# Shift of a folded batch normalisation: added by VectorE in PSUM in place of a product of ones

## What is computed

```
h = relu(bn1(conv1(x1)))          # conv1: 256x256, one tap; bn1: h * scale + shift, per feature
h = bn2(conv2(h))                 # 17 taps along the nodes, 256x256 each
x_conv = relu(h + x1)
```

## Time and profile before

| | us |
|---|---|
| median of 3 runs | 1957.12 |
| lowest, highest | 1956.53, 1961.15 |
| the profiled execution: time, span of the core | 1959.8, 1958.0 |

### The profile page before, as it was taken

How to read it: one execution, slowest core, us unless ns; L and a number is a source line. 1 busy time by engine, 2 the same in 40 slices (tenths; PEclk the granted TensorE clock), 3 DMA queues, 4 the chain that set the end, 5 groups by cost and what they waited for, 6 DMA issues and landing times.

```text
span 1958.0 us, 35045 instructions
## 1 busy us (share of the span) xinstructions
PE 1883.0 (96%) x11046; PEld 1655.8 (85%) x11046; DVE 1430.3 (73%) x2972; ACT 1115.5 (57%) x2063; POOL 423.3 (22%) x378
## 2 busy tenths in 40 slices
PE   7999999996999899949999999999999999999997
PEld 6988999996999799948888888888888888888886
DVE  5888888885666788856777777777777777777774
ACT  6888888884666677734444444444444444444442
POOL 4766766764454100000000000000000000000000
PEclk9999999997999899969999999999999999999998
DMA  6778888875334688852121211212121212121200
GB/s 220 269 270 287 292 293 293 304 249 193 96 102 145 204 287 275 260 171 91 51 93 59 86 65 68 83 51 99 50 100 50 100 50 93 58 87 64 79 33 22
DMA packets 184169, 281.13 MB, mean 144 GB/s; under 512 B 14286, under 2 KB 126644, under 8 KB 179860
## 3 DMA queue, kind: packets, MB, share of 16 engines
q1 hardware_dynamic: 184084, 280.10, 42.3%
HBM read 178.60 MB, written 101.45 MB: 143 GB/s over the span
## 4 chain that ended last, share of the span: by engine, by line
PE 54%; issue 1%; DVE 1%; ACT 0%; DMA 0%; POOL 0%; POOLq 0%; ACTq 0%; SPq 0%; DVEq 0%
PE c_ps_g L1573 40%; PE c_ps_m L1551 5%; PE c_ps_m L1582 2%; PE c_ps_y L1606 1%; PE c_ps_m L1584 1%; PE c_ps_y L1666 1%; PE c_ps_m L1666 1%; PE c_ps_m L1583 1%; PE c_ps_s L1651 0%; PE c_ps_y L1667 0%; PE c_ps_m L1667 0%; DMA c_x<-x_t 0%; PE c_ps_s L1620 0%; PE c_ps_g L1623 0%; DVE c_wi_l L1517 0%
## 5 line engine op out<-in xcount | busy, mean ns | idle before, releaser
L1333 POOL TENSOR_TENSOR c_rstd<-c_var_eps,c_neg_half 128x4 f32<-128x4 f32 x32 | 32.2, 1007 | 1059.5 <-DVE c_var_eps L1473 1059.5
L1251 ACT ACTIVATE c_yo<-c_ps_y,c_shift,c_rstd 128x256 f32<-128x256 f32 x128 | 61.8, 563 | 169.4 <-DVE c_shift L1481 169.4
L1573 PE MATMUL c_ps_g<-c_ch,c_wi_l 128*128 128x512 f32 x384 | 154.5, 402 | 0.0
L1573 PE MATMUL c_ps_g<-c_nh,c_wi_l 128*128 128x512 f32 x384 | 153.3, 399 | 0.0
L1573 PE MATMUL c_ps_g<-c_xh,c_wh_l 128*128 128x512 f32 x384 | 152.3, 397 | 0.0
L1573 PE MATMUL c_ps_g<-c_xl,c_wh_h 128*128 128x512 f32 x384 | 152.1, 396 | 0.0
L1573 PE MATMUL c_ps_g<-c_xh,c_wh_h 128*128 128x512 f32 x384 | 151.7, 395 | 0.0
L1573 PE MATMUL c_ps_g<-c_ch,c_wi_h 128*128 128x512 f32 x384 | 151.7, 395 | 0.0
L1573 PE MATMUL c_ps_g<-c_cl,c_wi_h 128*128 128x512 f32 x384 | 151.6, 395 | 0.0
L1573 PE MATMUL c_ps_g<-c_nl,c_wi_h 128*128 128x512 f32 x384 | 151.2, 394 | 0.0
L1573 PE MATMUL c_ps_g<-c_nh,c_wi_h 128*128 128x512 f32 x384 | 150.9, 393 | 0.0
(11 more groups left out here) (219 smaller groups left out, 6143.1 us busy)
## 6 DMA issues: line engine op xcount, KB each, us to landing
w_spec<-a_spec SPq DMA_DIRECT2D x32, 1088.0 KB, 8.0
m_w<-w_spec SPq DMA_DIRECT2D x34, 1024.0 KB, 8.1
a_xt<-in_x_t SPq DMA_DIRECT2D x64, 256.0 KB, 3.4
a_xn<-in_x_n SPq DMA_DIRECT2D x64, 256.0 KB, 5.1
x_t<-a_x1t SPq DMA_DIRECT2D x64, 256.0 KB, 4.8
s_x<-x_t SPq DMA_DIRECT2D x64, 256.0 KB, 2.9
y_spec<-x_spec SPq DMA_DIRECT2D x64, 256.0 KB, 5.5
c_x<-x_t SPq DMA_DIRECT2D x32, 512.0 KB, 3.9
```

The lines of the kernel that those rows point to most:

```text
L1251: nc.scalar.activation(yo[:, b], ps_y[:, b], ACT.Identity, bias=shift[:, b:b + 1], scale=rstd[:, b:b + 1]).then_inc(s_yo, 1)
L1573: last = nc.tensor.matmul(out, stationary, moving, start=(count == 0), stop=(count == total - 1))
```

## The change

The product of ones is taken out. The first of conv1's twelve products now opens the bank (`start=True`), the others add to it. When conv1 of a unit is done, VectorE adds the shift, kept in float32 on all partitions in a tile of its own and broadcast over the two graphs, to the unit's bank in PSUM, in place, and signals a new semaphore `s_sh`; ScalarE's relu waits for that instead of for conv1. The addition is the first thing in VectorE's step, for unit i-2, ahead of the sums of unit i-4 and of `hl` of unit i-2. The preparation of the rows in `phase_a` falls away; the copy that made the rounded part now makes the kept tile.

```diff
@@ def kept(keep)
-    shift_rows = keep[:, 2 * half:3 * half].rearrange("p (b d) -> p b d", b=2).bitcast(F32R)
-    f = keep[:, 3 * half:3 * half + 2 * L].rearrange("p (s l) -> p s l", s=2).bitcast(F32R)
-    ones = keep[:, 3 * half + 2 * L:3 * half + 2 * L + P].bitcast(F32R)
-    return w_h, w_l, shift_rows, f, ones
+    f = keep[:, 2 * half:2 * half + 2 * L].rearrange("p (s l) -> p s l", s=2).bitcast(F32R)
+    return w_h, w_l, f
@@ phase_a, tiles (shift_h, shift_l, shift_m go)
@@ phase_a, scalar
                 if i == 18:
                     act.wait_ge(s_ch, 1)
-                    nc.scalar.activation(shift_h[:, :], rows[:, 1], ACT.Copy).then_inc(s_ch, 1)
+                    nc.scalar.activation(shift_kept[:, :], rows[:, 1], ACT.Copy).then_inc(s_ch, 1)
...
                 if i == 22:
                     nc.scalar.activation(f[:, 0], f_raw[:, :], ACT.Copy).then_inc(s_ch, 1)
-                    nc.scalar.activation(ones_kept, ones0[:, :], ACT.Copy)
@@ phase_a, vector
-                if i == 20:
-                    dve.wait_ge(s_ch, 2)
-                    nc.vector.tensor_tensor(shift_l[:, :], rows[:, 1], shift_h[:, :].bitcast(F32), ALU.subtract).then_inc(s_cn, 1)
...
-                if i == 24:
-                    nc.vector.tensor_scalar(shift_m[:, :], shift_h[:, :].bitcast(F32), mk[:, 0:1], None, ALU.mult).then_inc(s_cn, 1)
-                if i == 25:
-                    dve.wait_ge(s_cn, 10)
-                    for b in range(2):
-                        nc.vector.scalar_tensor_tensor(shift_rows[:, b], shift_l[:, :], mk[:, 1:2], shift_m[:, :], ALU.mult, ALU.add).then_inc(s_cl, 1)
@@ phase_spectrum
-        w_h, w_l, shift_rows, f, ones = kept(keep)
+        w_h, w_l, f = kept(keep)
...
+        s_sh = sem("shift_added")
@@ phase_spectrum, scalar
                 if live(2):
                     p, r = i - 2, (u - 2) % RING
-                    reached(act, s_c1, p + 1)
+                    reached(act, s_sh, p + 1)
                     reached(act, s_f, B * (p - 1))
                     nc.scalar.activation(hh[:, u % 2], ps_c[:, r], ACT.Relu).then_inc(s_hh, 1)
@@ phase_spectrum, vector
             def step(i, u, k, live):
+                if live(2):
+                    p, r = i - 2, (u - 2) % RING
+                    reached(dve, s_c1, p + 1)
+                    nc.vector.tensor_tensor(ps_c[:, r], ps_c[:, r], shift.rearrange("p (o d) -> p o d", o=1).to_broadcast([P, B, D]),
+                                            ALU.add).then_inc(s_sh, 1)
                 if live(4):
                     p = i - 4
@@ phase_spectrum, tensor
                     reached(pe, s_xl, p + 1)
                     reached(pe, s_hl, p - RING + 1)
-                    nc.tensor.matmul(ps_c[:, r].rearrange("p b d -> p (b d)"), ones,
-                                     shift_rows.rearrange("p b d -> p (b d)"), start=True, stop=False)
...
-                            last = nc.tensor.matmul(ps_c[:, r, b], xx[:, v, c, nodes], ww[:, c], start=False,
+                            last = nc.tensor.matmul(ps_c[:, r, b], xx[:, v, c, nodes], ww[:, c], start=(b == 0 and t == 0),
                                                     stop=(b == B - 1 and t == len(passes) - 1))
@@ kernel
         keep = ctx.enter_context(nc.sbuf_tensor("keep", [P, 8 * D], F32))
+
+        shift = ctx.enter_context(nc.sbuf_tensor("s_shift", [P, D], F32))
```

More of the change, by code:

```diff
@@ L63, in kept, with phase_a @@
     w_l = keep[:, half:2 * half].rearrange("p (c o) -> p c o", c=KD).bitcast(F32R)
-    shift_rows = keep[:, 2 * half:3 * half].rearrange("p (b d) -> p b d", b=2).bitcast(F32R)
-    f = keep[:, 3 * half:3 * half + 2 * L].rearrange("p (s l) -> p s l", s=2).bitcast(F32R)
-    ones = keep[:, 3 * half + 2 * L:3 * half + 2 * L + P].bitcast(F32R)
-    return w_h, w_l, shift_rows, f, ones
-def phase_a(nc, G, x_n, x_t, adj_t, w0, b_t, masks, x1_t, taps, taps_s, dft_w, w_spec, w_c1, bn1, dft_f, keep, s_spec, s_out, first_x, s_x):
+    f = keep[:, 2 * half:2 * half + 2 * L].rearrange("p (s l) -> p s l", s=2).bitcast(F32R)
+    return w_h, w_l, f
+def phase_a(nc, G, x_n, x_t, adj_t, w0, b_t, masks, x1_t, taps, taps_s, dft_w, w_spec, w_c1, bn1, dft_f, keep, shift_kept, s_spec, s_out, first_x, s_x):
     pairs = G // 2
@@ L118, in phase_a @@
         diag = sb("diag", [P, 2, KD, P])
-        shift_h = sb("shift_h", [P, D], F32R)
-        shift_l = sb("shift_l", [P, D])
-        shift_m = sb("shift_m", [P, D])
         f_raw = sb("f_raw", [P, L])
-        c_h, c_l, shift_rows, f, ones_kept = kept(keep)
+        c_h, c_l, f = kept(keep)
         rows = diag.rearrange("p s c n -> p s (c n)")
@@ L664, in load_filters, with phase_spectrum @@
                  ).then_inc(s_w[buffer], 16)
-def phase_spectrum(nc, G, x1_t, keep, x_spec, s_spec, s_out, x, s_x, w, w_spec, s_w):
+def phase_spectrum(nc, G, x1_t, keep, shift, x_spec, s_spec, s_out, x, s_x, w, w_spec, s_w):
     B = 2
@@ L1792 @@
         phase_a(nc, G, d["x_n"], d["x_t"], d["adj_t"], d["w0"], d["b_t"], d["masks"], x1_t, d["taps"], taps_s, d["dft_w"], w_spec,
-                d["w_c1"], d["bn1"], d["dft_f"], keep, s_spec, s_out, x, s_x)
+                d["w_c1"], d["bn1"], d["dft_f"], keep, shift, s_spec, s_out, x, s_x)
         x_spec = ctx.enter_context(nc.sbuf_tensor("x_spec", [P, KD, SLOTS, 2, G], F32))
         w = ctx.enter_context(nc.sbuf_tensor("m_w", [P, PAIRS, KD, CHUNKS, 2, 2, CW], F32))
-        phase_spectrum(nc, G, x1_t, keep, x_spec, s_spec, s_out, x, s_x, w, w_spec, s_w)
+        phase_spectrum(nc, G, x1_t, keep, shift, x_spec, s_spec, s_out, x, s_x, w, w_spec, s_w)
         phase_product(nc, G, x_spec, w, w_spec, y_spec, y_rest, keep, x, s_w)
```

## The result

The changed kernel takes 2040.89 us (median of 4, 2040.22 to 2041.82) against 1958.18 before (median of 4, one execution more than in the table of the kernel before): a ratio of 1.0422, 95% interval 1.0406 to 1.0439. It is slower by 82.7 us, and lies inside the predicted range. The profiled execution took 2041.13 us.

The account below looks back on a forecast made before the run. PE was taken to bound the kernel. 62 units x 1.48 us = 91.8, less 0.6 for the other two, gave +91 us: 1959.8 + 91 = 2051 profiled, median 2048, range some 2024 to 2063, top carried to 2078.

Parts of the forecast that it names:

- PE sets the pace, the others have room: Spectrum stage: PE is busy in all 40.00 us of each window, DVE and ACT in some 26.5, POOL in 19.5.
- The added wait: PE stands still from conv1's end to the b=0 sum's end, behind DVE's addition: about 125 waits, some 95 us.
- Steps 1 and 2: From conv1's first product to the addition's start, 1.71 us; from there to the first sum's start, 0.61 us.
- the strict reading: DVE's sum would start only after all 0.69 us of the addition, adding an estimated 5 us.
- Step 3: From the first sum's start to the transform product that waits for it, 0.75 us.
- Step 5: Transform's b=1 waits for the second sum, about 0.55 us behind the first; then 0.48 to the next unit.
- The unit: One unit of the spectrum stage on PE takes 4.10 us, against 2.62 before: +1.48 us.
- The addition: DVE's added 128x512 operation, PSUM and SBUF in, takes 0.69 us.
- `phase_a`: Five small operations go from the preparation, on DVE and ACT: taken as 0, at most 2 us of gain.
- Rival A: PE's pauses in each unit lower its clock too: 5.5 us a unit, +179 us, 2137 us; chance 0.12.
- Rival B: Sums not behind the addition, or a second PE buffer: only the product is lost, 18 us gain, 1939 us; chance 0.05.
- Rival C: With sums free, the chain addition, relu, `hl` makes PE late, taking back the 0.28: about 1957 us; chance 0.05.

Follow-up runs that it names:

- The first kernel: The changed kernel with VectorE's addition moved behind the two sums of the same step: 1988.83 us, ratio 1.0146 to the kernel before.
- the second operation: The changed kernel with another full-size VectorE operation (PSUM plus shift into a spare tile) ahead of the addition: 2173.32 us, ratio 1.1092 to the kernel before.

## Why the prediction was right, point by point

- *PE sets the pace, the others have room.* Right, but room in total was not room in order: DVE had a third of its time free and held PE up all the same.
- *The added wait.* Right in kind: PE behind L760. There were 63 waits with 82.6 us, where about 125 with 95 us were expected: the second sum, for b=1, delays its product by 0.10 us (0.53 for 0.43), but shows as no wait of its own. TensorE was busy in 67% of a window, not near 60%. The first kernel shows that the order causes it.
- *Steps 1 and 2, 1.71 and 0.61 us.* Measured 1.71 and 0.61. The 1.71 was met by luck, in two halves that cancel: conv1 takes 1.28 us from its first row to its last in place of 1.19, and VectorE starts 0.43 us behind the last row, where ScalarE took 0.52. So VectorE's latency is not ScalarE's. The next operation started 0.61 us after one of 0.70, so the strict reading of the Trainium skill ("VectorE: DVE Perf Modes", The DRAIN you can't avoid) doesn't hold for this pair, and its 5 us were not there.
- *Step 3, 0.75 us.* The main term that was mis-sized: 0.67, or 62 x 0.08 = 5 us too much. It rested on one event at the stage's end.
- *Step 5, 0.55 + 0.48.* Measured 0.53 + 0.48.
- *The unit, 4.10 against 2.62 us.* Over 61 intervals the additions stand 3.99 us apart (474.62 to 718.0, units 2 to 63), the products of ones before 2.64 (473.73 to 635.05). The unit that I read before, 2.62, was one of the short ones: of four units in a row two take 2.60 to 2.63 and two 2.67 to 2.69. Afterwards three take 3.95 to 3.98 and one 4.05 or more. 61 x 1.35 = 82 us.
- *The addition, 0.69 us.* 0.700. Writing to PSUM in place cost nothing extra.
- *`phase_a`, nothing.* The stage's first product starts at 466.3 us in place of 466.7, 0.4 us of gain.
- *Rival A, the clock.* It did not happen, with less than 0.34 us to spare. My pause was 1.48 us; the real one 1.31. The clock fell at 1.65, so the 0.12 was a bet, not a finding. Its price was too low besides: 5.5 us a unit at half clock, where the 6.61 measured less 0.61 for the second operation leaves 6.0. The transform takes 1.83 us there (568.25 to 570.08), not 1.36.
- *Rival B, 18 us of gain.* The order-free price was too high: removing the product alone gave 9, as `xl` comes next, and 0.06 of the 0.28 us went to conv1's first product. It took two changes of order to get 14.
- *Rival C, about 1957 us.* Its condition was built, and it came out at 1989: the chain counted the addition, relu and `hl`, but not that VectorE can't do its sums while it waits inside that chain.

## What to carry to other kernels

Before work is moved to an engine with time to spare, write down what stands behind it in that engine's program order and who waits for that; an operation at the head of a step whose input comes at the end of the step delays everything behind it. Price a new wait as start to start along the whole ring, from conv1 back to conv1, and read the pace over many units. A moved operation often needs its consumers one step later: here the same change was worth +83 us in one order and -14 in another.

## What the runs showed that I had not expected

A pause of 1.31 us in a unit of 4.0 us left TensorE at 2.4 GHz, one of 1.65 us did not. A VectorE operation of 256 columns, both inputs and output in SBUF, then cost 100 us: 30 by its own time, as it took about 1 us in place of 0.34 in the eleven units where it ran beside GpSimd's `xl`, and 70 with the clock. And two waits of one step can be exchanged against each other with no change in time (1950.90 and 1951.54 us).
